# A macaron block on one core: first norm shared out otherwise, a wait moved, more idle transposes, and the constant rows of the attention buffers written by GpSimd between its scatters

## What is computed

```
x = x + 0.5 * ffn(layernorm(x))
x = x + attn(layernorm(x))          # 16 heads of 8
x = x + 0.5 * ffn(layernorm(x))

def ffn(x):
    indices = argmax(softmax(x @ Wr + br))       # one of 8 experts for each token
    for i in range(8):
        xi = x * (indices == i)                  # tokens of other experts become zero rows
        h = relu(xi @ W1[i] + b1[i])             # 128 -> 512
        out = out + (h @ W2[i] + b2[i])          # 512 -> 128
```

## Time and profile before

| | |
|---|---|
| median of 3 runs | 999.02 us (997.89 to 1002.86) |
| the profiled execution | 1000.25 us, of which the span of the records is 998.4 us |
| busy in the span | PE 92%, DVE 83%, ACT 75%, POOL 22% |
| mean granted TensorE clock | 0.968 of full |
| front up to source_i | 0 to 44.7 us |
| first FFN, first gather to last scatter | 45.5 to 138.4 us |
| attention begins (x back in) | 142.6 us |
| second FFN's last scatter | 991.94 us |

### The profile page before, as it was taken

The page is one execution under the profiler, slowest core; times in us unless marked ns, Lnnn a source line. Parts: engine busy times, 40 slices in busy tenths (PEclk is TensorE's granted clock), DMA queues, the critical chain, the costliest instruction groups (busy, mean ns, idle before and its releaser), DMA issues. The chain is left out here.

```text
span 998.4 us, 17986 instructions
## 1 busy us (share of the span) xinstructions
PE 918.1 (92%) x5975; PEld 382.3 (38%) x5975; DVE 829.9 (83%) x1396; ACT 752.1 (75%) x1509; POOL 217.3 (22%) x315
## 2 busy tenths in 40 slices
PE   3789966889999999999999999999999999965996
PEld 2689853422222222222222222222222222434996
DVE  6766558979999999999999999999999998768664
ACT  3367636878888888888888888888888888754774
POOL 5157631841000001000000100000100000024775
PEclk9789988989999999999999999999999999996998
DMA  8624535842220203202022120220202000051321
GB/s 265 184 86 120 160 108 191 257 168 63 63 60 17 62 30 85 61 18 62 15 72 75 31 62 15 72 54 28 75 30 64 30 22 17 1 170 48 104 64 43
DMA packets 68130, 78.67 MB, mean 79 GB/s; under 512 B 13088, under 2 KB 45512, under 8 KB 68040
## 3 DMA queue, kind: packets, MB, share of 16 engines
q1 hardware_dynamic: 61464, 64.52, 22.2%
q0 software_dynamic: 5120, 12.59, 4.1%
q10 hardware_dynamic: 1456, 0.41, 0.2%
HBM read 40.47 MB, written 33.49 MB: 74 GB/s over the span
## 5 line engine op out<-in xcount | busy, mean ns | idle before, releaser
L1561 DVE TENSOR_REDUCE maxima<-ps_m 128x2 f32<-128x1024 f32 x512 | 602.6, 1220 | 58.2 <-PE ps_m L1324 56.3
L1531 ACT ACTIVATE probs<-ps_s 128x512 f32<-128x512 f32 x1024 | 555.9, 599 | 109.1 <-PE ps_s L1370 78.7
L1370 PE MATMUL ps_s<-q,k 74*128 74x512 bf16 (+1 forms) x1024 | 312.1, 386 | 3.0 <-ACT probs L1531 3.0
L1381 PE MATMUL ps_o<-probs,vs 128*32 128x512 f32 x2048 | 273.6, 606 | 0.7 <-ACT probs L1531 0.7
L1370 PEld LDWEIGHTS ps_s<-q,k 74*128 74x128 bf16 (+1 forms) x1024 | 79.6, 97 | 307.1 <-ACT probs L1531 219.1
L1324 PE MATMUL ps_m<-k,q 64*128 64x512 bf16 x1024 | 160.1, 386 | 5.1 <-DVE maxima L1561 4.0
L1254 POOL TENSOR_SCALAR split<-top 128x16 bf16<-128x16 f32 x32 | 8.1, 253 | 443.0 <-DVE top L1577 429.3
L690 PE MATMUL ps_y<-W,hT 128*128 x624 | 86.4, 281 | 3.4 <-DVE hT L846 2.1
L1324 PEld LDWEIGHTS ps_m<-k,q 64*128 64x128 bf16 x1024 | 48.9, 93 | 102.3 <-issue 57.0
L1381 PEld LDWEIGHTS ps_o<-probs,vs 128*32 128x32 f32 x2048 | 40.3, 108 | 109.7 <-issue 94.7
L690 PEld LDWEIGHTS ps_y<-W,hT 128*128 128x128 f32 x624 | 78.1, 195 | 5.3 <-issue 5.1
(11 more groups left out here) (213 smaller groups left out, 571.7 us busy)
## 6 DMA issues: line engine op xcount, KB each, us to landing
k_rows<-parts SPq DMA_DIRECT2D x24, 384.0 KB, 4.4
sums<-oT SPq DMA_DIRECT2D x30, 256.0 KB, 2.1
q<-q_parts SPq DMA_DIRECT2D x75, 96.0 KB
k<-k_rows SPq DMA_DIRECT2D x15, 288.0 KB
token_rows<-x SPq DMA_DIRECT2D x16, 256.0 KB, 3.8
token_rows<-v_and_ctx SPq DMA_DIRECT2D x16, 256.0 KB, 4.1
k<-k_rows SPq DMA_DIRECT2D x15, 256.0 KB
q_parts<-parts SPq DMA_DIRECT2D x8, 384.0 KB, 3.4
```

What stands on the lines that cost most here:

```text
L1370: nc.tensor.matmul(ps_s[n % 3][:, :], k2[buffer(g)][0:contracted, j, kt * P:(kt + 1) * P], q2[buffer(g)][0:contracted, j, u * HALF:(u + 1) ...
L1381: last = nc.tensor.matmul(ps_o[32 * j:32 * (j + 1), :], vs[buffer(g)][:, kt, j, :], probs[:, s % 2, j, :], start=(kt == 0), stop=(kt == KT ...
L1531: nc.scalar.activation(probs[:, s % 2, j, :], ps_s[n % 3][:, :], ACT.Exp, scale=SCALE).then_inc(exped, 1)
L1561: nc.vector.tensor_reduce(maxima[:, :, pr, qt, kh], ps_m[slot][:, :, :], AX.X, ALU.max).then_inc(unit_free[slot], 1)
```

## The change

It has six parts.

1. **Norm split.** ScalarE normalises quads 0, 1 and 2 (before 0, 2 and 7), GpSimd 3 and 6 (before 1, 3 and 5), VectorE 4, 5 and 7 (before 4 and 6).
2. **Wait.** TensorE waits for the 11 small loads ahead of the first logits, no longer ahead of the idle turns.
3. **Idle turns.** 8 more behind each of the first four turned quads and 16 more ahead of `count`.
4. **Idle rows.** Six experts' idle products stand ahead of `find` (before four), two behind it. ScalarE takes the second copy of them ahead of its first `weights`; VectorE does the sum behind `relu(0)` and the writing of the others' sums behind `relu(1)`.
5. **Fill.** `sync_fill` and its constant tiles go. GpSimd writes each of the 12 pieces with a memset of 1024 float32 in each partition (pairs of bfloat16 ones as one float32), one behind each of the scatters 0 to 11.
6. **Second front.** The last quad's root stands ahead of the first logit copy on ScalarE.

```diff
-    def sync_fill(self, sp):
-        ...
-            sp.dma_start(self.k2[p][64:96, 0::2, :], constant(1, slice(64, 96))).then_inc(self.filled, 16)
-            sp.dma_start(self.k2[p][0:64, 1::2, :], constant(1, slice(0, 64))).then_inc(self.filled, 16)
-            sp.dma_start(self.q2[p][0:64, 1::2, :], constant(0, slice(0, 64))).then_inc(self.filled, 16)
+    FILLED = 4 * BUFS
+    def gpsimd_fill(self, pool, n):
+        p, piece = n // 4, n % 4
+        if n:
+            pool.wait_ge(self.filled, n)
+        if piece == 0:
+            self.nc.gpsimd.memset(self.k2[p][64:96, 0::2, :].bitcast(F32), self.PAIR).then_inc(self.filled, 1)
+        if piece == 1:
+            self.nc.gpsimd.memset(self.k2[p][0:64, 1::2, :].bitcast(F32), self.PAIR).then_inc(self.filled, 1)
+        if piece == 2:
+            self.nc.gpsimd.memset(self.q2[p][0:64, 1::2, :].bitcast(F32), 0.0).then_inc(self.filled, 1)
+        if piece == 3:
+            self.nc.gpsimd.memset(self.vs[p][:, :, :, :], 1.0).then_inc(self.filled, 1)
...
-        self.small_loaded(pe)          # end of tensor_biases
-    EARLY = EXPERTS // 2
+    EARLY, BANK = EXPERTS - 2, EXPERTS // 2
...
-    BY_ACT, BY_POOL = (0, 2, QUADS - 1), (1, 3, QUAD + 1)
+    BY_ACT, BY_POOL = (0, 1, 2), (3, QUAD + 2)
...
         for q in range(QUAD + 1):
             turn(q)
+            if q < QUAD:
+                self.setup.tensor_turns(pe, self.route.ps_lT, 8)
+        self.setup.small_loaded(pe)
         self.route.logits(pe, 0)
...
         self.route.turn_logits(pe, 1)
+        self.setup.tensor_turns(pe, self.route.ps_lT, 16)
         self.route.count(pe)
...
         for t in range(TILES):
             scatter(t)
+            if self.setup and t < self.setup.FILLED:
+                self.setup.gpsimd_fill(pool, t)
...
         self.list_items(dve)
+        relu(0)
         if self.setup:
             self.setup.vector_total(dve)
-        relu(0)
-        if self.setup:
+            relu(1)
             self.setup.vector_rest(dve)
-        relu(1)
...
-                tiles.setup.sync_fill(sp)
...
+                norm_2.root(act, last_span, 1)
                 route.copied_logits(act, 0)
-                norm_2.root(act, last_span, 1)
```

More of the change, by code:

```diff
@@ L128, in __init__ @@
         self.biases, self.total = sb("biases", [P, D], F32), sb("total", [P, D], F32)
-        self.blank = sb("blank", [P, 2, SEQ], BF16)
-        self.units = sb("units", [P, 2 * P], F32)
+        self.units = sb("units", [P, P], F32)
         self.iota_i = sb("iota_i", [P, P], I32)
@@ L180, in gpsimd_masks @@
         nc.gpsimd.memset(self.units[:, :], 1.0).then_inc(self.made, 1)
-        nc.gpsimd.memset(self.blank[:, 0, :], 0.0).then_inc(self.made, 1)
-        nc.gpsimd.memset(self.blank[:, 1, :], 1.0).then_inc(self.made, 1)
-    FILLED = 16 * 4 * BUFS
-    def sync_fill(self, sp):
[L188 to L192, removed]
-            sp.dma_start(self.k2[p][64:96, 0::2, :], constant(1, slice(64, 96))).then_inc(self.filled, 16)
-            sp.dma_start(self.k2[p][0:64, 1::2, :], constant(1, slice(0, 64))).then_inc(self.filled, 16)
-            sp.dma_start(self.q2[p][0:64, 1::2, :], constant(0, slice(0, 64))).then_inc(self.filled, 16)
-            sp.dma_start(self.vs[p][:, :, :, :].rearrange("p t j c -> p (t j c)").rearrange("p (a c) -> p a c", c=2 * P),
-                         self.units[:, :].unsqueeze(1).to_broadcast([P, KT * GH * 32 // (2 * P), 2 * P])).then_inc(self.filled, 16)
+    FILLED = 4 * BUFS
+    PAIR = float(0x3f803f80 - 0x3f800000) / 2 ** 23 + 1.0
+    def gpsimd_fill(self, pool, n):
[10 more added lines that the diff above has]
+            self.nc.gpsimd.memset(self.vs[p][:, :, :, :], 1.0).then_inc(self.filled, 1)
     def tensor_biases(self, pe):
@@ L251, in scalar_idle @@
         self.nc.scalar.activation(self.biases[:, :], self.ps_bias[:, 0:D], ACT.Copy).then_inc(self.idle_out, 1)
-        self.nc.scalar.activation(self.idle[:, 0:self.EARLY, :], self.ps_idle[:, 0:self.EARLY, :], ACT.Copy).then_inc(self.idle_out, 1)
+        self.nc.scalar.activation(self.idle[:, 0:self.BANK, :], self.ps_idle[:, 0:self.BANK, :], ACT.Copy).then_inc(self.idle_out, 1)
     def scalar_idle_late(self, act):
         act.wait_ge(self.idle_done, 2)
-        self.nc.scalar.activation(self.idle[:, self.EARLY:, :], self.ps_idle[:, self.EARLY:, :], ACT.Copy).then_inc(self.idle_out, 1)
+        self.nc.scalar.activation(self.idle[:, self.BANK:, :], self.ps_idle[:, self.BANK:, :], ACT.Copy).then_inc(self.idle_out, 1)
     RESTED = 3
@@ L512, in scalar @@
         normalise(0)
+        normalise(1)
+        self.norm.root(act, (QUAD * QUAD, TILES), 1)
         normalise(2)
-        self.norm.root(act, (QUAD * QUAD, TILES), 1)
         for q in range(QUADS):
-            if q == QUAD:
-                normalise(QUADS - 1)
             self.route.copied(act, q)
@@ L745, in relu @@
             last.then_inc(self.h_act, 1)
+        if self.setup:
+            self.setup.scalar_idle_late(act)
         act.wait_ge(self.listed, self.NAMED)
@@ L752, in scalar @@
             first.append(weights(i))
-        if self.setup:
-            self.setup.scalar_idle_late(act)
         relu(0)
@@ L863, in vector @@
         self.list_items(dve)
+        relu(0)
         if self.setup:
             self.setup.vector_total(dve)
-        relu(0)
-        if self.setup:
+            relu(1)
             self.setup.vector_rest(dve)
-        relu(1)
+        else:
+            relu(1)
         self.mask_items(dve)
```

## The result

The changed kernel takes 1002.41 us (median of 7 executions, 1000.73 to 1006.03), the kernel before in the same set 999.36 us (7 executions, 997.34 to 1002.86). The ratio is 1.004, with a 95% interval of 1.0023 to 1.0057. That is 3 to 4 us slower: clear of 1, and within the 5 us that the prediction counts as no change. The forecast was 1001.2. The profiled execution took 1000.73 us (span 998.8). It is the shortest of the seven, and 0.48 us over the profiled one before.

A forecast was written before the change was run, and what follows sets the result against it. GpSimd's scatters with the memsets were to set the end: -3.4 (start of the scatters) + 12.0 (memsets) - 5.8 (old slack) - 0.6 (second front) = +2.2 us, on the median of 999.02 giving 1001.2 us; range 996 to 1006.5.

The forecast's parts named there:

- slack: GpSimd's scatters behind scatter 0: 31 in a row would have taken 40.2 us and took 45.9, so 5.8 us spare.
- Front: From the idle turns to the second logits: earlier turns bring these logits at 27.1 instead of 28.49, 1.4 us earlier.
- Idle rows at the full clock: TensorE's 24 idle products ahead of `find`: about 5.1 us at full clock, the eight extra ones hidden, `find` not late.
- Rival D: Clock at half under the 24 products or the turns: `find` 2.4 us late, sum +4.6 to +5.6, time 1004; chance 0.1.
- First items: The first `down` waits no longer for VectorE: 52.0 instead of 55.49, 3.4 us earlier with the front's 1.4 in it.
- Scatter 0: GpSimd's first scatter moves with the items' 3.4 us gain, from 91.51 to 88.1.
- Memset: Each of GpSimd's 12 memsets behind the scatters adds 1.0 us, 12.0 in all.
- B: Memsets cost less; under 0.4 us each needed to gain 5 us; time 989 to 994, chance 0.08.
- C: Memset and indirect transfer cost more side by side: +5.2 us at 1.25 each, +7.0 at 1.4; time 1004 to 1006; chance 0.17.
- The last scatter: GpSimd's last scatter of the first FFN starts at 140.3 instead of 137.45, 2.8 us later.
- Second front: The last quad's turn starts once ScalarE has copied quad 5, 0.6 us earlier (0 to 1.4), and all behind it too.
- the 6.0 us: In the items, while SyncE issues the fills, TensorE starts 57 matmuls too few in 16 us, 6.0 us at that rate.

The follow-up runs named there:

- old_idle_rows: The changed kernel with part 4 undone (four experts' idle products ahead of `find`, VectorE's sum ahead of `relu(0)`): 1001.96 us, ratio 1.0026 to the kernel before.
- no_new_turns: The changed kernel without part 3, so without the added idle turns: 1002.08 us, ratio 1.0031 to the kernel before.
- fills_thrice: The changed kernel with three memsets instead of one behind each of scatters 0 to 11 (36 in all): 1024.33 us, ratio 1.0258 to the kernel before.
- before_early_fills: The kernel before with SyncE's fill replaced by GpSimd's twelve memsets, all ahead of the gathers: 994.01 us, ratio 0.9944 to the kernel before.

## Why the prediction was right, point by point

The class came out, and so did the size: +2.2 us forecast, +0.5 in the profiled execution, +3.05 between the medians. The bound was the right one: GpSimd's chain of scatters and memsets ends the first FFN, with 5.8 us of slack to start from. But the +2.2 was to come from a last scatter 2.8 us later, and the profile has it 0.45 us earlier (137.00 against 137.45). Two terms of the sum were too pessimistic. With the measured sizes it is -4.7 (scatter 0) + 10.3 (memsets) - 5.8 (slack) - 0.6 = about -0.8, a little faster and not slower. That the medians lie near the forecast is therefore luck in good part (see "Open" below).

- **Front: forecast 1.4 earlier, measured 2.6.** The chain was built step by step with about 1.1 us for eight idle turns. They ran at 141 ns a load ('s lower row), the next real turn followed 0.9 us behind their start, and ScalarE's copies gate the third turn (18.64, behind `xnT`). But 2.6 is one profile against one. Over all profiles `source_i` lies at 43.16 to 45.41 with the old front (four, mean 44.1) and at 41.47 to 42.68 with the whole new one (eight, mean 42.2), so the gain is nearer 1.9. It varies with the arrival of x and of the small loads.
- **What the step in the earlier trace rows is.** The prediction read 231 ns, then 141, as the clock coming up. The granted clock in the profile reads 1.00 through both, so the step alone doesn't prove it; old_idle_rows does.
- **Idle rows at the full clock, `find` not late: right.** 5.62 us for 24 products (forecast 5.1), and `find` waits 0.85 for ScalarE. Rival D's lower clock is what no_new_turns shows (8.23), but not its price of 2.4 us: the clock was full again before the products ended, and `find` ended with VectorE's columns all the same.
- **First items: forecast 3.4 with the front's 1.4 in it (the rows give 3.5), so about 2.0 beyond it; measured 3.9 with 2.6, so 1.3.** The 1.27 of old_idle_rows is this term. `down` no longer waits for VectorE but for its own place behind `up` of the second item and the transposed tile (51.38 + 0.21). The missing 0.7 has a source that the prediction put at nothing: with two experts instead of four behind `find`, TensorE runs out of work at 45.1, and from 48 on the clock is at its half. From `up` of the second item to the transposed tile it then takes 1.86 us (49.52 to 51.38), where it took 0.99 (52.12 to 53.11). In old_idle_rows, with four experts behind `find` again, the clock is full from 46 to 52 and the same stretch takes 0.99 (50.36 to 51.35).
- **Scatter 0: forecast 88.1, measured 86.79.** I carried over the gain of the first `down` alone. The result of item 0 comes 3.45 us earlier (55.67 against 59.12), but items 1 and 2 follow 1.2 and 1.8 us behind where they took 2.7 and 2.0, since VectorE's writing into W no longer stands ahead of them: the third result is 5.1 earlier, and the gathers and scatter 0 (4.7 earlier) follow it. In old_idle_rows, where the spacing is 2.7 and 2.0 again, scatter 0 is at 89.75, earlier than before only by what `source_i` is.
- **Memset: forecast 1.0, measured 0.86 between scatters,** 1.7 us less in all. The gap that I let it pay in full is mostly shared. Rivals B (under 0.4) and C (1.25 and up) are refuted.
- **The last scatter: forecast 140.3, measured 137.00.** The 3.3 us are the two terms above (1.3 and 1.7), and 0.3 because 31 spacings took 39.9 and not 40.2.
- **Second front: forecast 0.6 earlier, measured 0.1, and not kept.** The quad's four turns start at 890.63 instead of 890.75, with the rows ahead of them 0.27 later than before (VectorE's `shift_a` at 880.20 against 879.93), so the reordering itself gave 0.4. They wait 0.34 for ScalarE's copy. `source_i` comes 0.14 earlier and the last gather 0.25 (950.25 against 950.50). Then GpSimd stands still for 1.07 us ahead of the first scatter, where it was 0.30, and names nothing that it waits for. So the scatters begin at 952.27 against 951.80 and end 0.4 late (992.34 against 991.94). old_idle_rows has 1.16 at the same place, fills_thrice 0.30; what it is stays open.
- **What the items gained (10.8 us in the last result, forecast 9) went into the wait for GpSimd,** as forecast: TensorE idles 17.49 us ahead of the attention. The lull costs little besides: the granted clock is at its half up to 147 and the attention's first transposes take 1.01 instead of 0.66, but its second quad is turned at 150.19, against 150.33 before.

The removal of SyncE's fill works as told: 146 matmuls in 16 us, against 95, and before_early_fills shows it with the old front too. The Trainium skill, "SBUF — State Buffer", "Who interferes with whom", says that a transfer never contends with a compute engine. The prediction took the 6.0 us as evidence against that rule, which they are not. The instructions take the same time beside the fill as without it; what grows is the idle time between them. Here are the weight loads of `down` from 96 to 112 us (columns as in the earlier trace rows), in the kernel before and in before_early_fills:
```profile
L690 PEld LDWEIGHTS ps_y<-W,hT 128*128 128x128 f32 x47 | 6.2, 190 | 2.4 <-issue 2.4
...
L692 PEld LDWEIGHTS ps_y<-W,hT 128*128 128x128 f32 x71 | 8.6, 192 | 0.0
```
ScalarE's relu takes 366 ns in both and VectorE's 345 and 346. So the trace neither breaks the rule nor says what the engines wait for while the fill runs.

**Open.** The rows add up to a changed kernel no slower than before, the profiled spans to 0.4 us slower, the medians to 3. Two things are known of the difference. First, the profiled execution of the changed kernel is the fastest of its seven, while the one before is 0.9 us above its median, so the two profiles understate it. Second, the executions fall in two groups. Four of the seven lie at 1000.7 to 1002.4 and three at 1005.4 to 1006.0, the latter at a lower mean clock (0.958 against 0.960 to 0.965). In the last set the upper group has three of 29 in the kernel before (1004.1 to 1004.9, clock 0.964 against 0.967 to 0.974), four of 12 in before_early_fills (996.5 to 999.1 against 991.2 to 994.5), four of 12 in no_new_turns and three of 12 in old_idle_rows. A mean clock lower by 0.006 is about 12 us more at the half level, in which at most 6 us of TensorE's work would be missing: an estimate that fits the 4 to 5 us and shows no cause. Every profile is of the quicker executions. The grouping alone doesn't explain the 3 us either: the changed kernel's four quicker executions have a median of 1001.9, still 2.5 above the 999.36 before. On the other side, no_new_turns and old_idle_rows, by their profiles 2.1 and 1.7 us slower than the changed kernel, have ratios of 1.0031 and 1.0026, below its 1.004. So that the changed kernel is slower at all rests on seven executions whose interval leaves out 1, and the size of 3 us is not firm. Nor is it known what the engines wait for in the stalls of the first two sets.

## What to carry to other kernels

Before work is moved onto an engine that is 22% busy, ask how much slack its chain has at that place: here 5.8 us of it stood against 10.3 of memsets, while the same engine had over 20 us of waiting for `source_i` a stage earlier. Put fillers into the wait, not into the chain; the same twelve memsets there make the old kernel 0.56% faster. And a gain of 11 us in the items is worth nothing while the result leaves through a chain of 32 scatters at 1.29 us each that is busy from end to end. When a run with one part removed comes out later, follow the delay back to the first row that is late before giving it to that part: half of the 1.75 us of no_new_turns stood ahead of the first turn that had been taken out.

## What was not expected of the hardware

A GpSimd memset of 1024 elements takes 0.94 to 0.98 us on 32, 64 or 128 partitions, in float32 as in bfloat16 (0.946). By these rows the same bytes, written as half as many elements of twice the size, should take about half the time (an estimate; no run wrote these buffers as bfloat16). The gap ahead of an indirect transfer is 0.30 us behind another and 0.17 behind a memset. On one and the same chip the kernel before took 1052 us in one set and 1000 in another, with stalls of the items that the trace gives no local releaser for.
